# Who issues the shift copies of a convolution: SyncE in place of ScalarE in a Macaron state-space layer

## The chip, the cores and the metric

The kernel runs on one core of one Trainium2 chip. The metric is the device time of one execution in microseconds (us). A core has five engines that each work through an instruction list of their own, in order: TensorE (PE in the profile), VectorE (DVE), ScalarE (ACT), GpSimd (POOL) and SyncE (SP). They meet through semaphores. A DMA is issued by one of the engines; an engine's DMA issues stand in its own list, so a wait in front of a DMA holds up whatever is behind it on that engine.

## The reference

Input x has shape (2, 2048, 256), that is 4096 tokens of 256 channels. In short:

```
x = x + 0.5 * ffn(layernorm(x))      # 8 groups of 512 tokens, each with its own W1, b1, W2, b2; no nonlinearity
x = x + ssm(layernorm(x))
x = x + 0.5 * ffn(layernorm(x))

ssm(x): xz = x @ Wi.T + bi;  x_in, z = halves of xz (512 channels each)
        u  = silu(causal depthwise convolution of x_in with 4 taps + conv_b)
        dt = softplus(x_in[..., :32] @ Wdt.T + bdt)
        h  = h * exp(dt * A) + dt * Bm * u,  y = sum over 16 states of h * Cm     # along time
        out = (y * silu(z)) @ Wo.T + bo + x * Dv.mean()
```

## The kernel before

The tokens are cut into 4 iterations (`it`) of 1024 tokens, and the 512 channels into 4 tiles of 128 (`ct`). A block k = 4 * it + ct, from 0 to 15, is one tile of channels over one stretch of 1024 tokens. Block 0 is prepared in two halves of 512 tokens, and blocks 0 and 15 are scanned in two halves.

For each block the kernel makes these steps (stage names as in the code):

- `xim` on TensorE (x_in of the tile, two halves of 512 tokens in PSUM), `halo` and `xi` on ScalarE (three columns of the past, then bias and the copy into XI). XI has 128 partitions by two groups g of channels: group g fills the 64 partitions from 64 g on.
- `sh`: two DMAs that copy each group, shifted by one token, into the other 64 partitions of XI. So one matmul with a contraction over 128 partitions does two taps.
- `um` on TensorE (two taps at a time, DIAG as weights), `u` on ScalarE (silu). Likewise `zm` and `z`.
- `dm` on TensorE, `dtr`, `dte`, `dtl` on ScalarE and `dt` on VectorE make dt. `w` on VectorE makes dt * u. Both stand in DW.
- `repd` and `repw`: DMAs that spread a quarter q of the 128 channels over four times as many partitions, from DW to RD (dt) and to RV (dt * u). 512 KB each.
- 16 units per block, written (k, s), with the quarter q = s % 4: `exp` on ScalarE (G from RD), `scan` on VectorE (G from G and RV), and after each four scans `red` on TensorE (sum over states into Y). G has 8 buffers, so an exponential waits for the reduction of eight units earlier. `yz` on VectorE joins the block's Y with z.

Beside this run the norms (`sum`, `sq` and others), the FFN (the weights of each group are multiplied together first: `mm`, `ms`, `mv`, `mt`, `mtc`, with weights loaded by `wa`), the loads of X (`x`), the output projection (`opa`, `opm`, `op`) and the stores.

The order of all this is written by `schedule()`: a loop over the 288 units, with chains of steps that are let in at set points. It gives one list; each engine runs the stages of it that are its own, in that order. `proj(k)` puts `sh` in:

```
        do("xim", k, 1)
        yield 0
        do("xi", k, 1)
        do("sh", k)
        yield from rest_for(SHIFT)
```

Worked through, the list has these stages of SyncE on either side of `sh(k)` (w is repw, d is repd, numbers are block and quarter):

```
k    SyncE before            SyncE after
0    x(3)                    d(0), second half
1    w(0,3) second half      x(2), wa(20) to wa(27)
2    wa(27)                  d(1,0) to d(1,3), w(1,0) to w(1,3), wa(28) ...
3    w(2,1)                  w(2,2), w(2,3)
4    w(3,1), x(5)            w(3,2), w(3,3)
5    w(4,1)                  w(4,2), w(4,3)
6    w(5,1)                  w(5,2), w(5,3)
7    w(6,1), store(0)        w(6,2), w(6,3)
8    w(7,3)                  wa(52) to wa(59), w(8,0)
9    w(8,0)                  d(8,0) to d(8,3), w(8,1), wa(60) to wa(63), w(8,2)
10   w(9,1)                  w(9,2), w(9,3)
11   w(10,1), store(2)       w(10,2), w(10,3)
12   w(11,3)                 store(3), w(12,0)
13   w(12,1)                 w(12,2), w(12,3)
14   w(13,1)                 w(13,2), w(13,3)
15   w(14,1), store(4)       w(14,2), w(14,3)
```

On ScalarE `sh(k)` stands directly behind `xi(k,1)`. Behind `sh(1)` stands `sum(6)`, which reads x(2).

Of the kernel before, what the change touches and what calls it, by code (L numbers as in the profile page):

```python
# [12 lines left out]
TOK = 1024  # L13
# [39 lines left out]
HALVED, SPLIT = (0,), (0, 15)  # L53
# [37 lines left out]
def span(k, p):  # L91

    return (512 * p, 512 * p + 512) if k in HALVED else (0, TOK)
# [555 lines left out]
def build(nc, x, w, wit, wdt, wot, bo, cols, masks, out):  # L649
# [3 lines left out]
    with ctx:  # L653
        def sb(name, shape):
            return ctx.enter_context(nc.sbuf_tensor(name, shape, F32))
# [9 lines left out]
        XI = sb("XI", [P, 2, TOK + 3])  # L665
# [37 lines left out]
        sems = {name: ctx.enter_context(nc.semaphore("s_" + name)) for name in [*count.total, "skips", "mv1"]}  # L703
# [29 lines left out]
        def fourfold(v):  # L733

            return v.unsqueeze(1).broadcast_to([32, 4, v.shape[1]])

        def parts(i):

            k, p, s = UNITS[i]
            return k, p, s // 4, s % 4  # L740
# [19 lines left out]
        def scanned(k):  # L760

            return k, runs(k) - 1

        @block.sync
        def _(eng):
            e = Engine(eng, count, sems)

            def do(stage, *a):
                if stage == "x":
                    g, = a  # L770
                    if g >= NX:
                        e.wait_ge("store", g - NX)
                    eng.dma_start(X[:, g % NX, :, :], x[512 * g:512 * g + 512, :].rearrange("(i p) d -> p i d", p=P)
                                  ).then_inc(sems[DMA["x"](g)], 16)
                elif stage == "col":
                    eng.dma_start(COL[:, :], cols).then_inc(sems["col"], 16)
                elif stage == "mask":
                    eng.dma_start(MASKS, masks).then_inc(sems["mask"], 16)
                elif stage == "wdt":
                    eng.dma_start(WDT[:, :], wdt).then_inc(sems["wdt"], 16)  # L780
                elif stage == "bo":
                    eng.dma_start(BO[:, :], bo).then_inc(sems["bo"], 16)
                elif stage == "wi":
                    eng.dma_start(WI[:, :, :], wit.rearrange("(j p) n -> p j n", p=P)).then_inc(sems["wi"], 16)
                elif stage == "wo":
                    eng.dma_start(WO[:, :, :], wot.rearrange("(j p) n -> p j n", p=P)).then_inc(sems["wo"], 16)
                elif stage == "wh":
                    g, c = a
                    dst = heads[g][:, 513 * c:513 * (c + 2)].rearrange("p (k n) -> p k n", n=513)
                    eng.dma_start(dst, w[g].rearrange("(p k) n -> p k n", k=8)[:, c:c + 2, :]  # L790
                                  ).then_inc(sems[DMA["wh"](g, c)], 16)
                elif stage == "wa":
                    n, = a
                    if n - NW >= 16:
                        e.wait_ge("mm", n - NW)
                    eng.dma_start(W[:, n % NW, :], w[n // 8].rearrange("(p k) n -> p k n", k=8)[:, n % 8, :]
                                  ).then_inc(sems[DMA["wa"](n)], 16)
                elif stage == "store":
                    g, *part = a
                    pairs = part or (0, 1)  # L800
                    for pr in pairs:
                        e.wait_ge("ffn", g // 2, 1, g % 2, pr)
                    tiles = slice(2 * pairs[0], 2 * pairs[-1] + 2)
                    ov = out[512 * g:512 * g + 512, :].rearrange("(i p) d -> p i d", p=P)[:, tiles, :]
                    eng.dma_start(ov, X[:, g % NX, tiles, :]).then_inc(sems[DMA["store"](g)], 16)
                elif stage == "repd":
                    k, q, p = a
                    t0, t1 = span(k, p)
                    e.wait_ge("dt", k, p)
                    e.wait_ge("mm", 15)  # L810
                    if k:
                        e.wait_ge("exp", AT[(*scanned(k - 1), 12 + q)])
                    eng.dma_start(RD[:, q, t0:t1], fourfold(DW[q:P:4, 0, t0:t1])
                                  ).then_inc(sems[DMA["repd"](*a)], 16)
                elif stage == "repw":
                    k, q, p = a
                    t0, t1 = span(k, p)
                    e.wait_ge("w", k, p)
                    e.wait_ge("mm", 15)
                    n = 4 * k + q - NR  # L820
                    if n >= 0:
                        ko, qo = divmod(n, 4)
                        e.wait_ge("scan", AT[(*scanned(ko), 12 + qo)])
                    eng.dma_start(RV[:, (4 * k + q) % NR, t0:t1], fourfold(DW[q:P:4, 1, t0:t1])
                                  ).then_inc(sems[DMA["repw"](*a)], 16)
                elif stage == "end":
                    e.wait_ge("store", 6)
                    e.wait_ge("store", 7, 1)

            schedule(do)  # L830

        @block.gpsimd
# [68 lines left out]
        def _(eng):  # L901
            e = Engine(eng, count, sems)
            eng.preload_act_table_set("natural_log_exp_and_others")

            def do(stage, *a):
# [65 lines left out]
                elif stage == "ms":  # L971
                    g, = a
# [8 lines left out]
                elif stage == "mtc":  # L981
                    g, = a
# [44 lines left out]
                elif stage == "halo":  # L1027
                    k, = a
# [7 lines left out]
                elif stage == "xi":  # L1036
                    k, hf = a
# [6 lines left out]
                        ins = eng.activation(XI[ps, g, 3 + 512 * hf:515 + 512 * hf], bank("xim", k, hf)[ps, :],  # L1044
                                             ACT.Identity, bias=COL[ps, BI + k % 4:BI + k % 4 + 1])
                    ins.then_inc(sems["xi"])
                elif stage == "sh":
                    k, = a
                    e.wait_ge("halo", k)
                    e.wait_ge("xi", k, 1)  # L1050
                    c0 = 512 if k in HALVED else 0
                    for g in range(2):
                        eng.dma_start(XI[64 - 64 * g:128 - 64 * g, g, c0:TOK + 2],
                                      XI[64 * g:64 * g + 64, g, c0 + 1:TOK + 3]).then_inc(sems["sh"], 16)
                elif stage == "xd":
                    it, hf = a
                    ps = slice(32 * hf, 32 * hf + 32)
# [5 lines left out]
                elif stage == "u":  # L1063
                    k, hf = a
# [6 lines left out]
                elif stage == "z":  # L1071
                    k, hf = a
# [5 lines left out]
                elif stage == "dtr":  # L1078
                    k, hf = a
# [9 lines left out]
                elif stage == "dte":  # L1089
                    k, p = a  # L1090
# [6 lines left out]
                elif stage == "dtl":  # L1097
                    k, p = a
# [6 lines left out]
                elif stage == "save":  # L1105
                    i, = a
                    k, p, _ = UNITS[i]
# [3 lines left out]
                elif stage == "exp":  # L1111
                    i, = a
                    k, p, m, q = parts(i)
# [6 lines left out]
                    if o >= 0:  # L1120
                        e.wait_ge("red", o)
                        if kept(o):
                            e.wait_ge("save", o)
                    eng.activation(G[:, i % NG, t0:t1], RD[:, q, t0:t1], ACT.Exp,  # L1124
                                   scale=NAC[:, states(i):states(i) + 1]).then_inc(sems["exp"])

            schedule(do)

        @block.vector
# [376 lines left out]
```

## Time and profile before

| | |
|---|---|
| three timed runs, median | 760.28 us (758.97 to 765.12) |
| the profiled execution, its own time | 761.95 us |
| its span (first to last instruction) | 760.1 us |
| mean granted clock of TensorE | 0.926 of full |
| DMA issues of XI<-XI, all by ScalarE | 30 of 256.5 KB, 2 of 128.5 KB |
| DMA issues by SyncE | RD<-DW 68, RV<-DW 68, weights, X, stores |

All times of the trace are microseconds from the start of the span, from one execution. The line numbers are those of the kernel before.

### The profile page before, as it was taken

The page shows a single profiled execution, that of the slowest core. Times are in us where ns is not written, and L with a number is a line of the kernel's source. Part 1 is how long each engine was busy: PE and PEld are TensorE (multiplying, and loading weights), DVE is VectorE, ACT ScalarE, POOL GpSimd, SP SyncE. Part 2 cuts the span into 40 slices and gives each one's busy share as a digit, 9 for nine tenths or more (in the row PEclk, how much of TensorE's full clock was granted, in tenths as well). Part 3 has the DMA queues.
Part 4 walks back from the last instruction along what each step waited for, and adds up shares of the span by engine and source line. Part 5 has one row for each costly group of instructions (what it writes and reads, how often), then busy time and mean ns, then how long its engine had stood idle before and what let it go on. Part 6 is the DMA issues. An engine that isn't in the chain of part 4 may idle for free. (4 is left out here: it accounts for less than half of the span.)

```text
span 760.1 us, 8303 instructions
## 1 busy us (share of the span) xinstructions
PE 644.2 (85%) x2928; PEld 333.1 (44%) x2928; DVE 666.6 (88%) x450; ACT 607.4 (80%) x1074; POOL 293.8 (39%) x184
## 2 busy tenths in 40 slices
PE   7867786799896999979798999994977997798857
PEld 5632333364342466445144575531231553265435
DVE  2437947879999999999999999999999999999971
ACT  2488896879889989998788989898888787866663
POOL 0107020134344588479912565046970060600010
PEclk9997998989997899999899999997997999899879
DMA  8431465341838070431658070614234331605001
GB/s 294 148 138 43 164 225 164 133 172 32 320 104 315 7 245 5 160 117 49 227 150 301 34 236 0 231 47 166 84 146 132 139 111 71 206 28 221 1 1 55
DMA packets 40026, 103.08 MB, mean 136 GB/s; under 512 B 4080, under 2 KB 13040, under 8 KB 39984
## 3 DMA queue, kind: packets, MB, share of 16 engines
q1 hardware_dynamic: 37424, 94.40, 34.2%
q10 hardware_dynamic: 2560, 8.14, 4.6%
q8 instruction: 23, 0.38, 0.2%
q14 instruction: 19, 0.16, 0.1%
HBM read 23.08 MB, written 4.19 MB: 36 GB/s over the span
## 5 line engine op out<-in xcount | busy, mean ns | idle before, releaser
L1124 ACT ACTIVATE G<-RD,COL 128x1024 f32<-128x1024 f32 (+1 forms) x288 | 280.0, 1042 | 56.2 <-PE Y L1424 50.8
L1246 DVE TENSOR_TENSOR_SCAN G<-G,STT,RV 128x1024 f32<-128x1024 f32 (+1 forms) x160 | 312.5, 2016 | 1.5 <-ACT G L1124 1.5
L1246 DVE TENSOR_TENSOR_SCAN G<-G,RV 128x1024 f32<-128x1024 f32 (+1 forms) x128 | 268.7, 2155 | 13.9 <-ACT G L1124 13.8
L1424 PE MATMUL Y<-G,RW 128*32 128x512 f32 x1024 | 144.6, 682 | 49.4 <-DVE G L1246 46.1
L849 POOL TENSOR_SCALAR LV<-LV 128x4 f32<-128x4 f32 x18 | 17.3, 962 | 226.4 <-ACT XN L944 226.1
L858 POOL TENSOR_TENSOR LV<-LV,HALF 128x4 f32<-128x4 f32 (+1 forms) x25 | 47.8, 1913 | 135.8 <-DVE LV L1201 134.3
L1424 PEld LDWEIGHTS Y<-G,RW 128*32 128x32 f32 x1024 | 28.0, 117 | 127.6 <-DVE G L1246 64.6
L875 POOL TENSOR_SCALAR XN<-X,LV 128x256 f32<-128x256 f32 x36 | 75.9, 2113 | 1.9
L1391 PE MATMUL MB<-XI,DIAG 128*64 128x512 f32 x248 | 64.3, 656 | 12.7 <-DMA XI<-XI 10.8
L1350 PE MATMUL MB<-MT,XF 128*128 128x256 f32 x240 | 59.6, 393 | 9.9 <-ACT MT L986 7.6
L1369 PE MATMUL MB<-XT,WI 128*128 128x512 f32 x128 | 63.4, 624 | 3.7 <-ACT XT L970 3.7
L889 POOL TENSOR_SCALAR X<-X,LV 128x256 f32<-128x256 f32 x32 | 65.2, 2047 | 0.8
L1448 PE MATMUL MB<-WO,ZS 128*128 128x256 f32 x256 | 64.0, 383 | 0.0
L1402 PE MATMUL MB<-XT,WI 128*128 128x512 f32 x128 | 59.7, 615 | 4.0 <-ACT XF L970 2.6
L895 POOL TENSOR_SCALAR MS<-MS,MV 128x256 f32<-128x256 f32 x12 | 27.4, 2290 | 88.3 <-DVE MV L1178 88.3
L1350 PEld LDWEIGHTS MB<-MT,XF 128*128 128x128 f32 x240 | 46.9, 198 | 18.8 <-ACT MT L986 6.0
L1448 PEld LDWEIGHTS MB<-WO,ZS 128*128 128x128 f32 x256 | 49.3, 192 | 6.8
L1287 PE MATMUL MB<-W 128*128 128x257 f32 x192 | 47.8, 396 | 1.4 <-DMA W<-in_w 1.4
L944 ACT ACTIVATE XN<-X,LV 128x256 f32<-128x256 f32 x96 | 47.5, 498 | 1.6 <-DVE LV L1206 1.1
L1044 ACT ACTIVATE XI<-MB,COL 64x512 f32<-64x512 f32 x64 | 43.3, 676 | 3.5 <-PE MB L1369 3.1
L1287 PEld LDWEIGHTS MB<-W 128*128 128x128 f32 x192 | 35.5, 194 | 20.1 <-issue 10.5
L1194 DVE SCALAR_TENSOR_TENSOR DW<-MB,COL,DW 128x1024 f32<-128x1024 f32 (+1 forms) x18 | 20.5, 1143 | 25.1 <-ACT DW L1102 25.1
(96 smaller groups left out, 779.7 us busy)
## 6 DMA issues: line engine op xcount, KB each, us to landing
RD<-DW SPq DMA_DIRECT2D x60, 512.0 KB, 3.7
RV<-DW SPq DMA_DIRECT2D x60, 512.0 KB, 4.9
W<-in_w SPq DMA_DIRECT2D x48, 256.5 KB, 3.6
XI<-XI ACTq DMA_DIRECT2D x30, 256.5 KB, 5.6
X<-in_x SPq DMA_DIRECT2D x8, 512.0 KB, 6.3
out<-X SPq DMA_DIRECT2D x7, 512.0 KB, 3.3
G<-in_w SPq DMA_DIRECT2D x4, 513.0 KB, 8.4
RV<-in_w SPq DMA_DIRECT2D x4, 513.0 KB, 12.3
```

The source lines that it names most:

```text
L858: eng.tensor_tensor(lv[:, 3, ts], lv[:, 1, ts], HALF[:, ts], ALU.pow).then_inc(sems["rstd"])
L875: ins = eng.tensor_scalar(xn[:, i, :], v[:, i, :], lv[:, 3, i:i + 1], lv[:, 4, i:i + 1], ALU.mult, ALU.add)
L889: eng.tensor_scalar(v[:, i, :], v[:, i, :], lv[:, 5, i:i + 1], lv[:, 6, i:i + 1], ALU.mult, ALU.add).then_inc(sems["skip"])
L1124: eng.activation(G[:, i % NG, t0:t1], RD[:, q, t0:t1], ACT.Exp, scale=NAC[:, states(i):states(i) + 1]).then_inc(sems["exp"])
L1246: eng.tensor_tensor_scan(g, g, RV[:, (4 * k + q) % NR, t0:t1], STT[:, idx:idx + 1] if goes_on else 0.0, ALU.mult, ALU.add).then_inc(sems[" ...
L1287: ins = eng.matmul(bank("merge", g, i)[:, 0:257], v[:, 257 + 128 * i:385 + 128 * i], v[:, 0:257], start=(c == 0), stop=(c == 7))
L1350: ins = eng.matmul(o, xf[:, j, 128 * t:128 * t + 128], MT[:, g % NX, j, :], start=False, stop=(i == 1 and j == 1))
L1369: ins = eng.matmul(bank("xim", k, hf), WI[:, j, 128 * ct:128 * ct + 128], XT[:, j, 512 * hf:512 * hf + 512], start=(j == 0), stop=(j == 1))
L1391: ins = eng.matmul(bank("um", k, hf)[64 * g:64 * g + 64, :], DIAG[:, 4 * ct + 2 * g + t, :], XI[:, g, 512 * hf + 2 * t:512 * hf + 2 * t + ...
L1402: ins = eng.matmul(bank("zm", k, hf), WI[:, j, 512 + 128 * ct:640 + 128 * ct], XT[:, j, 512 * hf:512 * hf + 512], start=(j == 0), stop=(j ...
L1424: ins = eng.matmul(Y[32 * q:32 * q + 32, 512 * h:512 * h + 512], RW[:, states(i + o), :], G[:, (i + o) % NG, 512 * h:512 * h + 512], start ...
L1448: ins = eng.matmul(o, ZS[:, (4 * it + ct) % NZ, 128 * (2 * pr + i):128 * (2 * pr + i) + 128], WO[:, ct, :], start=False, stop=(i == 1 and ...
```

## The change

The stage `sh` moves from ScalarE's list to SyncE's, at the same place in the order. Its waits (`halo`, `xi`), its two DMAs, their sizes and their semaphore stay; no other stage changes.

```diff
         @block.sync  (do)
+                elif stage == "sh":
+                    k, = a
+                    e.wait_ge("halo", k)
+                    e.wait_ge("xi", k, 1)
+                    c0 = 512 if k in HALVED else 0
+                    for g in range(2):
+                        eng.dma_start(XI[64 - 64 * g:128 - 64 * g, g, c0:TOK + 2],
+                                      XI[64 * g:64 * g + 64, g, c0 + 1:TOK + 3]).then_inc(sems["sh"], 16)
         @block.scalar  (do)
-                elif stage == "sh":
-                    k, = a
-                    e.wait_ge("halo", k)
-                    e.wait_ge("xi", k, 1)
-                    c0 = 512 if k in HALVED else 0
-                    for g in range(2):
-                        eng.dma_start(XI[64 - 64 * g:128 - 64 * g, g, c0:TOK + 2],
-                                      XI[64 * g:64 * g + 64, g, c0 + 1:TOK + 3]).then_inc(sems["sh"], 16)
```

## Rows read from the trace of the kernel before

**Rows 1.** The page's first part: busy us (share of the span) xinstructions.

```profile
PE 644.2 (85%) x2928; PEld 333.1 (44%) x2928; DVE 666.6 (88%) x450; ACT 607.4 (80%) x1074; POOL 293.8 (39%) x184
```

**Rows 2.** Windows, 600 to 690 us: stretch, length, busy us of each engine, clock, DMA.

```profile
600.00:690.00 90.00, 80.76 (x380) 44.04 (x377) 90.00 (x47) 71.53 (x105) 25.62 (x12) 0.94 0.35 125
```

**Rows 3.** Timeline of VectorE: start, us, line, what, [idle before <-releaser].

```profile
104.15 1.28 DVE L1194 SCALAR_TENSOR_TENSOR DW<-MB,COL,DW 128x1024 f32<-128x1024 f32 x1 [10.19 <-ACT DW L1102]
...
118.45 8.84 DVE L1246 TENSOR_TENSOR_SCAN G<-G,RV 128x1024 f32<-128x1024 f32 x4 [4.78 <-ACT G L1124]
...
144.53 1.23 DVE L1233 TENSOR_TENSOR DW<-DW 128x1024 f32<-128x1024 f32 x1 [3.46 <-ACT DW L1069]
...
166.56 4.53 DVE L1246 TENSOR_TENSOR_SCAN G<-G,RV 128x1024 f32<-128x1024 f32 x2 [5.51 <-ACT G L1124]
...
352.80 4.59 DVE L1246 TENSOR_TENSOR_SCAN G<-G,STT,RV 128x1024 f32<-128x1024 f32 x2 [1.49 <-ACT G L1124]
```

**Rows 4.** The line that issues sh: ns min/median/max, first and last start.

```profile
L1053 ACTq DMA_DIRECT2D XI<-XI x32: 468/564/2587, 67.4 to 653.2; - x32
```

**Rows 5.** Timeline of SyncE's and ScalarE's issues and one sum, 80 to 114 us.

```profile
80.68 0.60 SPq L773 DMA_DIRECT2D X<-in_x  x1
...
92.78 1.12 ACTq L1053 DMA_DIRECT2D XI<-XI  x2
93.94 0.42 ACT L919 ACTIVATE XN<-X 128x256 f32<-128x256 f32 x1 [1.25 <-issue]
...
105.46 3.39 SPq L813 DMA_DIRECT2D RD<-DW  x4
...
113.75 3.08 ACTq L1053 DMA_DIRECT2D XI<-XI  x2
```

**Rows 6.** Issue to landing: X at 80.7, XI at 210.3, RD burst, XI at 113.7.

```profile
DMA to landing us min/median/max: 3.6/3.6/3.6
...
DMA to landing us min/median/max: 3.1/3.4/3.8
...
L813 SPq DMA_DIRECT2D RD<-DW x4: 530/706/1318, 105.5 to 107.5; - x4
DMA to landing us min/median/max: 3.0/4.2/4.8
...
DMA to landing us min/median/max: 6.5/7.9/9.4
```

**Rows 7.** Timeline of block 1: TensorE's um(2,0), ScalarE's exponentials of units 8 on.

```profile
123.73 3.68 PE L1391 MATMUL MB<-XI,DIAG 128*64 128x512 f32 x8 [6.13 <-DMA XI<-XI]
...
137.60 3.23 ACT L1124 ACTIVATE G<-RD,COL 128x1024 f32<-128x1024 f32 x3 [0.95 <-PE Y L1424]
```

**Rows 8.** Timeline around block 3: VectorE's scans, SyncE's RV, ScalarE's XI.

```profile
202.69 13.63 DVE L1246 TENSOR_TENSOR_SCAN G<-G,RV 128x1024 f32<-128x1024 f32 x6
...
202.95 1.82 SPq L824 DMA_DIRECT2D RV<-DW  x2
...
210.25 1.12 ACTq L1053 DMA_DIRECT2D XI<-XI  x2
```

**Rows 9.** Timeline around block 8: RD, XI, exponentials of units 0 to 3, dt.

```profile
399.45 3.59 SPq L813 DMA_DIRECT2D RD<-DW  x4
...
405.49 1.26 ACTq L1053 DMA_DIRECT2D XI<-XI  x2
...
408.55 4.27 ACT L1124 ACTIVATE G<-RD,COL 128x1024 f32<-128x1024 f32 x4 [1.15 <-PE Y L1424]
...
418.31 1.25 DVE L1194 SCALAR_TENSOR_TENSOR DW<-MB,COL,DW 128x1024 f32<-128x1024 f32 x1
```

**Rows 10.** Timeline around block 6: RV(6,2) and (6,3), XI, scan (6,2).

```profile
321.62 2.65 SPq L824 DMA_DIRECT2D RV<-DW  x2
...
325.52 1.41 ACTq L1053 DMA_DIRECT2D XI<-XI  x2
...
334.32 2.34 DVE L1246 TENSOR_TENSOR_SCAN G<-G,STT,RV 128x1024 f32<-128x1024 f32 x1
```

## The prediction

> **What bounds the kernel now.** The page's first part gives the busy shares: VectorE 88%, TensorE 85%, ScalarE 80% [rows 1]. The windows by stage say more than the average: from 600 to 690 us VectorE is busy for 90.00 of 90.00 us [rows 2]. It runs the 288 scans one behind the other, and a microsecond in which a scan is late there is a microsecond of the span. So I listed VectorE in order of time and looked for its gaps [rows 3]. Before the first full-width scan (block 1, at 118.45) there are large ones, 10.19 and 4.78 us. Inside block 1 there are 3.46 and 5.51 us. From 166.56 until after 690 us few are left, the largest 1.49 us at 352.80. That gives two rules for costing a delay. Up to 166 us it counts where it lies on the chain that ends a gap. After that it counts almost whole as soon as it reaches a scan.
>
> **What is moved.** 32 DMA issues of ScalarE, 0.468 to 2.587 us each, median 0.564 [rows 4]: 32 x 0.564 = 18 us of ScalarE's time at the least. The bytes, the two waits and the place in the order stay. What changes is the engine that stands still until `xi(k,1)` is done. ScalarE never stood still for it, for it makes XI itself. SyncE does, and everything queued behind `sh(k)` on SyncE stands with it: input tiles, weights, and the replications RD and RV from which ScalarE and VectorE live. So for each of the 16 pairs I took the time of the issue on ScalarE (XI is ready just before it) and laid it beside the time at which SyncE issued the next item of its own order. Where SyncE's item came earlier, it is now late by the difference plus the two issues. On ScalarE an undisturbed pair takes 1.12 us [rows 5]; I use 1.15.
>
> **Step 1, sh(1), in front of x(2).** SyncE issued x(2) at 80.68; XI is ready at 92.7, where ScalarE issues the pair (92.78), and the next thing ScalarE does is the sum over x(2), at 93.94 [rows 5]. Now x(2) is issued at 92.75 + 1.15 = 93.9. Alone it took 3.6 us to land, the XI pair 3.1 to 3.8 us from issue, and four 512 KB replications of one burst 3.0 to 4.8 us [rows 6]. The last of that burst landed at 107.5 + 4.8 = 112.3 and the first at 105.5 + 3.0 = 108.5, so each further 512 KB costs (112.3 - 108.5)/3 = 1.28 us. The second of the XI pair lands at 93.3 + 3.8 = 97.0, x(2) 1.28 us later at 98.3; with no such queueing at 93.9 + 3.6 = 97.5. ScalarE's sum starts at 98.3 instead of 93.94: 4.4 us late (3.6 to 6). All that follows on ScalarE up to the dt step of block 1 is without a gap, and VectorE stands in its 10.19 us gap waiting for just that [rows 3]. So +4.4 goes to everything behind. The weights wa(20) to wa(27) also move behind x(2), but TensorE needs them some 2 us before ScalarE's late chain needs their product: nothing, and 1 to 2 us if that cover is thin.
>
> **Step 2, sh(2), in front of the replications of block 1.** In the frame of the old times (all 4.4 us later): SyncE issued repd(1) at 105.46 and XI is ready at 113.66, the pair being issued at 113.75 [rows 5]. Now the pair goes at 113.7, repd(1,0) at 114.9. The second XI lands at 114.2 + 3.8 = 118.0, and repd(1,0) to (1,3) and repw(1,0) follow in the same queue: 118.0 + 5 x 1.28 = 124.4, and 126.5 if the queue is a third slower under such a load (1.7 us each). The first scan of block 1 needs repw(1,0), so it starts at 124.4 and not at 118.45. Most of this has cover. Block 1 has gaps of 3.46 and 5.51 us, 9 us together, and they hang on another chain: TensorE waited 6.13 us for the late landing of sh(2), and ScalarE's exponentials of units 8 to 11 began at 137.60 [rows 7]. The pair meets no other traffic now and lands 5 us earlier, so TensorE and its weight products are early. What releases those exponentials then is the scans: four (8.84 us), the yz product (1.17), the reduction on TensorE (2.0) behind the first scan's start, so 124.4 + 12.1 = 136.5, or 138.6 at the upper bound, against 137.60. The next group, eight scans in, gives 146.6 to 148.8 against 147.2. So block 2 starts 0.6 us earlier to 1.6 us later: I take +0.5. ScalarE's long issue there (3.08 us for the pair) is gone too, but it lay under this wait.
>
> **Step 3, sh(4), in front of repw(3,2).** SyncE issued repw(3,2) at 202.95; the pair was issued at 210.25 [rows 8]. Now repw(3,2) goes at 211.4. VectorE's run of six scans from 202.69 holds the last two of block 2 and the first four of block 3, at 2.27 us each [rows 8], so scan (3,2) starts at 202.69 + 4 x 2.27 = 211.8. Its operand lands 1.28 us after the second XI (214.5 + 1.3 = 215.8), at the least 211.4 + 3.0 = 214.4 (the quickest of the burst [rows 6]). VectorE stands for 2.6 to 4.0 us: +3.5, nearer to the upper end, since the pair is always just ahead in the queue. There is no gap near it to take this up.
>
> **Step 4, sh(9), in front of repd(8).** repd(8) was issued from 399.45 on and the pair at 405.49 [rows 9]. Now repd(8,0) goes at 406.65, and the four land at about 411.0 to 414.9. ScalarE's exponentials of units 0 to 3, begun at 408.55, end one exponential (1.07 us) behind the last landing, at 416.0 instead of 412.8. The dt chain of block 9 behind them takes 3.5 us and ends at 419.5, where VectorE took it up at 418.31 [rows 9]: 1.2 us, or nothing if the four land 1.2 us sooner. +1.0.
>
> **The other twelve.** In seven of them (k = 0, 6, 8, 10, 12, 13, 14) SyncE has nothing due before XI is ready. For k = 3, 5, 7, 11 and 15 a repw (.,2) is late by 0.2 to 5 us. The tightest is k = 7: repw(6,2) at 321.62 becomes 326.65, for the pair went at 325.52. It lands at 331.4, and scan (6,2) starts at 334.32 [rows 10]: 2.9 us of cover, and 3 to 10 us in the other four. Nothing; if ScalarE were 3 us later against the scans, each microsecond beyond would count.
>
> **What ScalarE gets back.** Its 18 us lie mostly in front of waits for TensorE's reduction, which come from the scans. They count where ScalarE itself ends a gap of VectorE: 1.49 us at 352.80 [rows 3], on a stretch without waits behind the pair of 325.52 (1.41 us [rows 10]), and smaller gaps at 502 and 507, 1.2 us together. At most 2.7 us; I take half: -1.4.
>
> The Trainium skill, "DMA: Bandwidth & Descriptors", section "Issuing engines are not separate DMA queues", says that DMAs of scalar, sync and gpsimd all run on the same 16 engines and interleave, and that another issuer only saves issue time on a sequencer. The landing of 9.4 us for sh(2) beside a SyncE burst, against 3.8 for sh(4) [rows 6], agrees with the sharing. By that rule alone only the term of ScalarE's issue time would stand and the sum would be slightly negative, which is the second rival below; the rule is silent on the items behind a blocked sequencer.
>
> **The sum.** 4.4 + 0.5 + 3.5 + 1.0 - 1.4 = 8.0 us. Span 760.1 + 8.0 = 768.1 us. The profiled execution took 761.95 us, 1.85 more than its span, and lies 1.7 us above the median of the three timed runs (760.28); added to the median the change gives 768.3 us, +1.05%. About 1% is what a measurement of this kernel can tell from no change, so the forecast lies on that bound.
>
> **Rivals.**
> Absorbed: the first delay hides. ScalarE, TensorE and VectorE are all idle for parts of the stretch up to 166 us, and if x(2) lands sooner or block 1's gaps (9 us) take up step 1 as well, steps 1 and 2 come to 0 to 2 us. With step 3: +2 to +4, 762 to 764 us. For: the gaps are large. Against: ScalarE's chain from 93.94 is closed.
> Relief, the other side: SyncE's blocking costs nothing and ScalarE's 18 us come back. This decides if the operands on which steps 1 and 3 rest are not waited for, that is if XI is ready before about 89 us for x(2) and 207 us for repw(3,2). Then -1.4 to -2.7 us from the gaps that ScalarE ends, 757.6 to 759 us; up to -8 if the exponentials run ahead everywhere. Against: in this trace XI is ready at 92.7 and 210.2.
> Cascade: each stall leaves TensorE idle too, the granted clock falls, and blocks behind it run late, so that repw(6,2) and its like lose their 3 us. Block 1 at the upper bounds (+1.6), step 1 at 6, another 3 us at one more block: +13 to +18, 773 to 778 us.
>
> **Chances.** As worked out (764 to 773 us) 0.63; absorbed 0.17; cascade 0.13; relief 0.07. The range to hold 8 in 10 reaches from the absorbed case to the lower half of the cascade, 762.5 to 775. Slower by over 1% (above 767.9) is half of the main case and a bit, and the cascade: 0.50. Faster by over 1% is a small part of the relief: 0.04. The rest, 0.46, is within 1%.
>
> **What would show it.** Right: x(2) issued near 93.9 and a wait of ScalarE for the DMA of X in front of the sum; the first scan of block 1 at about 129 with block 2 starting near 171; a gap of VectorE of 3 to 4 us in front of scan (3,2), which ends with a DMA of RV; near 352.8 a smaller gap. Wrong: if XI is ready sooner on SyncE's side than on ScalarE's old place, if a single queue drains faster or slower than 1.28 us for 512 KB, or if a later block loses its cover.

## The result and the profile after

The changed kernel takes 781.15 us (median of 4 runs) against 761.19 us before: ratio 1.0254, 95% interval 1.0207 to 1.0301. It is 2.5% slower. The forecast was 768.3 us, in a range of 762.5 to 775. Medians, here and below, are of all executions; ratios leave out those more than 1.5% above the fastest of their kernel (two of these ran at a granted clock of 0.81 and 0.82 instead of about 0.93). The profiled execution has a span of 778.9 us, 18.8 more than before.

The first part of the page of the kernel after, and its DMA queue of SyncE, beside [rows 1]:

```profile
PE 650.3 (83%) x2928; PEld 337.1 (43%) x2928; DVE 667.3 (86%) x450; ACT 609.0 (78%) x1074; POOL 295.5 (38%) x184
...
q1 hardware_dynamic: 39984, 102.54, 37.3%
```

VectorE's work is the same (667.3 us for 666.6). What grew is its idle time. SyncE's queue now carries the pairs too: 102.54 MB and 37.3% of the engines' span, where it was 94.40 MB and 34.2%. The waits of SyncE's own queue say where to look (what waited, for what, us in total, times, longest):

```profile
SPq L181 <- ACT XI L1052: 94.4, 13, 19.8
```

Line 181 is the wait of the stages, so SyncE stood for 94.4 us in front of `sh`, in 13 waits. The question is which of it anybody else felt. VectorE in order of time, kernel after, beside [rows 3]:

```profile
113.78 1.28 DVE L1194 SCALAR_TENSOR_TENSOR DW<-MB,COL,DW 128x1024 f32<-128x1024 f32 x1 [18.96 <-ACT DW L1102]
134.75 8.84 DVE L1246 TENSOR_TENSOR_SCAN G<-G,RV 128x1024 f32<-128x1024 f32 x4 [11.45 <-DMA RV<-DW]
...
224.70 4.47 DVE L1246 TENSOR_TENSOR_SCAN G<-G,RV 128x1024 f32<-128x1024 f32 x2 [4.40 <-DMA RV<-DW]
...
433.78 4.48 DVE L1246 TENSOR_TENSOR_SCAN G<-G,RV 128x1024 f32<-128x1024 f32 x2 [0.70 <-DMA RV<-DW]
451.17 4.71 DVE L1246 TENSOR_TENSOR_SCAN G<-G,RV 128x1024 f32<-128x1024 f32 x2 [1.64 <-ACT G L1124]
...
478.42 1.41 DVE L1194 SCALAR_TENSOR_TENSOR DW<-MB,COL,DW 128x512 f32<-128x512 f32 x2 [1.43 <-ACT DW L1102]
485.10 1.22 DVE L1255 TENSOR_TENSOR ZS<-ZS,Y 128x1024 f32<-128x1024 f32 x1 [2.42 <-PE Y L1424]
```

The four places of the prediction are there. The gap in front of dt(1) grew from 10.19 to 18.96 us. The first scan of block 1 waits for RV (11.45 us), and the two gaps inside block 1, 3.46 and 5.51 us before, have shrunk to nothing and 0.75. The gap in front of scan (3,2) is 4.40 us. The surprise is the third stretch: from block 8 into block 9 there are six gaps, 7.5 us together, where the kernel before has one of 1.16.

To cost them I numbered the 288 scans in both profiles (a merged row of n scans divided evenly) and took, for each, how much later it starts than in the kernel before. The differences of this column between two places are what the stretch costs. All runs stand here, in us against the first profile of the kernel before:

| start of scan, later than before by | block 0, 2nd half | its unit 11 | block 1 | block 2 | block 4 | block 8 | block 10 | block 15, 2nd half |
|---|---|---|---|---|---|---|---|---|
| after (all by SyncE) | 0.8 | 9.6 | 16.3 | 8.2 | 12.9 | 12.8 | 19.2 | 17.4 |
| the kernel before again | 2.3 | 2.9 | 2.9 | 2.8 | 2.9 | 3.8 | 3.5 | 3.6 |
| only sh(1) | 2.3 | 10.7 | 8.9 | 7.8 | 7.9 | 10.6 | 10.4 | 10.5 |
| only sh(2) | -0.1 | 0.4 | 6.7 | -2.2 | -1.9 | -2.2 | -2.2 | -2.3 |
| only sh(4) | 0.2 | 0.7 | -1.1 | -1.3 | 5.2 | 5.0 | 4.8 | 4.8 |
| only sh(9) | -2.0 | -2.0 | -2.5 | -2.2 | -2.2 | -1.1 | 5.3 | 5.6 |
| the other twelve | -1.0 | -0.1 | -1.8 | -2.7 | -2.7 | -2.8 | -3.0 | -4.8 |
| SyncE waits only | -0.4 | 7.1 | 13.7 | 5.6 | 9.9 | 8.0 | 16.6 | 16.0 |
| x(2) first | -2.6 | 3.3 | 10.0 | 1.9 | 8.5 | 6.4 | 12.5 | 10.6 |
| x(2), wa(20) to wa(23) first | 1.5 | 1.4 | 7.7 | -0.8 | 4.1 | 3.8 | 10.2 | 8.2 |
| sh(9) behind RD | 2.1 | 2.7 | 0.9 | 0.8 | 0.9 | -1.9 | -2.1 | -2.2 |
| by SyncE, in the order of readiness | 0.2 | -0.3 | -3.2 | -2.3 | -2.3 | -4.3 | -3.2 | -4.9 |

Read along a row, not down a column: the first column is what the start-up happened to take in that execution (-2.6 to +2.3 us), before anything changed has an effect. In the kernel after the start-up took 0.8 us more, the stretches cost 8.8 us (sh(1)), -1.4 (sh(2)), +4.7 (sh(4)), 0, +6.4 (sh(9)) and -1.8, and the last blocks add 1.4 to the span's 18.8.

### The profile page after: what moved, and what is told of

Read it like the earlier page. It is cut to its first block and busy times, and to the rows that moved or that the text cites. A ratio compares the mean times of both kernels' runs of the same rounds, so it can differ in the third digit from the quotient of the medians.

```text
span 778.9 us, 8303 instructions
## 1 busy us (share of the span) xinstructions
PE 650.3 (83%) x2928; PEld 337.1 (43%) x2928; DVE 667.3 (86%) x450; ACT 609.0 (78%) x1074; POOL 295.5 (38%) x184
## 3 DMA queue, kind: packets, MB, share of 16 engines
q1 hardware_dynamic: 39984, 102.54, 37.3%
## 5 line engine op out<-in xcount | busy, mean ns | idle before, releaser
L1424 PE MATMUL Y<-G,RW 128*32 128x512 f32 x1024 | 146.7, 691 | 57.8 <-DVE G L1246 53.1
L866 POOL TENSOR_TENSOR LV<-LV,HALF 128x4 f32<-128x4 f32 (+1 forms) x25 | 45.7, 1830 | 138.6 <-DVE LV L1201 137.1
L897 POOL TENSOR_SCALAR X<-X,LV 128x256 f32<-128x256 f32 x32 | 70.6, 2217 | 0.8
L1391 PE MATMUL MB<-XI,DIAG 128*64 128x512 f32 x248 | 61.1, 628 | 8.1 <-DMA XI<-XI 4.6
L903 POOL TENSOR_SCALAR MS<-MS,MV 128x256 f32<-128x256 f32 x12 | 30.2, 2526 | 98.2 <-DVE MV L1178 98.2
L1287 PE MATMUL MB<-W 128*128 128x257 f32 x192 | 54.4, 436 | 12.9 <-DMA W<-in_w 12.9
L883 POOL TENSOR_SCALAR XN<-X,LV 128x256 f32<-128x256 f32 x36 | 64.0, 1783 | 1.9
L1287 PEld LDWEIGHTS MB<-W 128*128 128x128 f32 x192 | 39.7, 216 | 33.6 <-DMA W<-in_w 17.4
```

The lines of the kernel that those rows point to most:

```text
L883: ins = eng.tensor_scalar(xn[:, i, :], v[:, i, :], lv[:, 3, i:i + 1], lv[:, 4, i:i + 1], ALU.mult, ALU.add)
L897: eng.tensor_scalar(v[:, i, :], v[:, i, :], lv[:, 5, i:i + 1], lv[:, 6, i:i + 1], ALU.mult, ALU.add).then_inc(sems["skip"])
L1287: ins = eng.matmul(bank("merge", g, i)[:, 0:257], v[:, 257 + 128 * i:385 + 128 * i], v[:, 0:257], start=(c == 0), stop=(c == 7))
L1391: ins = eng.matmul(bank("um", k, hf)[64 * g:64 * g + 64, :], DIAG[:, 4 * ct + 2 * g + t, :], XI[:, g, 512 * hf + 2 * t:512 * hf + 2 * t + ...
L1424: ins = eng.matmul(Y[32 * q:32 * q + 32, 512 * h:512 * h + 512], RW[:, states(i + o), :], G[:, (i + o) % NG, 512 * h:512 * h + 512], start ...
```

## The experiments

**One place at a time.** A constant says which pairs SyncE issues; the rest stay with ScalarE.

```diff
+BY_SYNC = (1,)          # and (2,), (4,), (9,), or the twelve others
 @block.sync
+                elif stage == "sh" and a[0] in BY_SYNC:
 @block.scalar
-                elif stage == "sh":
+                elif stage == "sh" and a[0] not in BY_SYNC:
```

> Only sh(1) by SyncE, the other fifteen by ScalarE as before. Theory A (the items queued behind the blocked SyncE cost the time, x(2) and the weights wa(20) on): x(2) is issued near 94 to 96 us, ScalarE waits about 5 to 6 us for it in front of the sum and about 3 us for the reduction behind late weights, and the scan of unit 11 of block 0's second half starts about 9 us later than before; of that some 4 to 8 us reach the end of the span. Rival B (it is the traffic of all sixteen pairs in SyncE's one DMA queue that slows every landing): one pair alone does next to nothing, under 2 us. Rival C (the gaps of block 1 take the delay up): 9 us at unit 11, but 0 to 2 us at the start of block 2 and at the end.

> Only sh(2) by SyncE. Theory A: the first scan of block 1 starts 6 to 7 us later than before, and the start of block 2 lies within -1.5 to +1.5 us of before, because the gaps of 3.5 and 5.5 us in block 1 hang on the landing of sh(2), which comes 5 us sooner. Total -1.5 to +1.5 us. Rival C (a late first scan of block 1 goes to the end whole): +6 to +7 us. Rival B: under 1 us anywhere.

> Only sh(9) by SyncE. Theory A: RD of block 8 is issued 6 to 7 us late, the weight loads wa(60) to wa(63) reach the queue 1 to 2 us late and TensorE waits about 4 to 5 us for them in front of a reduction; VectorE loses 4 to 6.5 us between the start of block 8 and unit 4 of block 9. Rival (as predicted blind: only the dt step of block 9 is late): +1 us. Rival B: under 1 us.

> All pairs but 1, 2, 4 and 9 by SyncE. Theory A: no operand of a scan is late, and the relief of ScalarE shows where ScalarE ended a gap of VectorE (1.5 us at 352.8, 1.2 us near 502 to 507): -3 to 0 us against before. Rival B (traffic in one queue): several us slower, in proportion to the twelve pairs, 5 to 9 us. Rival (a later block loses its cover, such as repw(6,2) with 2.9 us): +1 to +3 us in that block.

> Only sh(4) by SyncE. Theory A: repw(3,2) is issued 8 to 9 us later, VectorE waits 3.5 to 4.5 us for it in front of unit 2 of block 3, and all of it reaches the end, since no gap lies near: +3.5 to +4.5 us against the same place of the kernel before. Rival C (taken up by later gaps): under 1.5 us at the end.

| by SyncE | this, us | before, us | ratio (95%) |
|---|---|---|---|
| only sh(1) | 771.58 | 760.70 | 1.0140 (1.0069 to 1.0211) |
| only sh(2) | 759.68 | 760.70 | 0.9998 (0.9962 to 1.0033) |
| only sh(4) | 767.66 | 762.47 | 1.0076 (1.0036 to 1.0116) |
| only sh(9) | 773.49 | 760.70 | 1.0175 (1.0088 to 1.0261) |
| the other twelve | 759.23 | 760.70 | 0.9974 (0.9942 to 1.0006) |

Three of sixteen pairs make the whole loss. sh(1) costs 8.4 us at unit 11 in the table and 8.2 at the end, sh(9) 6.4 and sh(4) 6.5 where they lie. The twelve, with three quarters of the traffic, are no slower: against the theory that one queue for everything is what costs.

sh(2) delays the first scan of block 1 by 6.4 us and still leaves block 2 2.6 us earlier than it would have been. That it gains anything is not shown, though. From the same unit 11 to block 2 kernels that leave sh(2) with ScalarE are ahead too, by 2.9 us (only sh(1)), 2.6 (the other twelve), 2.0 (only sh(4)) and 1.9 (sh(9) behind RD), and only sh(9) and the second profile of the kernel before are not (0.2 and 0.1). What goes with it is the length of ScalarE's second issue of that pair: 2.59 and 2.56 us in the two profiles of the kernel before, 2.02 with only sh(9), 0.72 to 0.79 in the other four. What makes it long is not shown. sh(2) on SyncE costs nothing; that much stands.

Three expectations missed. sh(1) came to 10.9 us in the timed runs, where 4 to 8 were expected. sh(9) came to 12.8, where 4 to 6.5 were expected; its profile, with 5.1 us more span than the first of the kernel before, is of the fastest of its four executions (766.99 us, the others 771.90 to 775.37), so 5 to 8 us of the others' time are in no trace. And sh(4) costs 6.5 where it lies; I expected 3.5 to 4.5, the size in the kernel after. The profile of only sh(4) shows what the size hangs on:

```profile
203.55 4.27 ACT L1133 ACTIVATE G<-RD,COL 128x1024 f32<-128x1024 f32 x4 [4.63 <-PE Y L1433]
...
211.13 1.15 SPq L813 DMA_DIRECT2D XI<-XI  x2
...
212.33 1.95 SPq L833 DMA_DIRECT2D RV<-DW  x2
...
217.05 4.47 DVE L1255 TENSOR_TENSOR_SCAN G<-G,RV 128x1024 f32<-128x1024 f32 x2 [6.42 <-DMA RV<-DW]
```

ScalarE's exponentials waited 4.63 us for the reduction, where they waited 3.15 in the kernel before and after. XI of block 4 stands behind them, so the pair went 2.0 us later against the scans (0.5 us behind the end of the last one, in the kernel after 1.5 us ahead of it), and the gap was 6.42 us instead of 4.40. The 1.5 us of the wait are TensorE's clock. In all three kernels it stands idle for 2.68 us in front of the four matmuls ahead of that reduction; they take 1.95 and 1.96 us in the kernel before and after, at a granted clock of 1.00 (2.4 GHz), and 3.44 us with only sh(4), at 0.55 (most of it at the lower level, 1.2 GHz). With x(2) first (below) it is the same: 2.87 us for the four and 2.65 for the reduction (1.92 otherwise), a wait of 4.79 and a gap of 6.30. What decides the level there is open. The price of a blocked queue moves one for one with the engine that releases it.

**The wait alone.** SyncE waits at the sixteen places, and ScalarE issues the pairs as before.

```diff
 @block.sync
+                elif stage == "sh":
+                    e.wait_ge("halo", *a)
+                    e.wait_ge("xi", *a, 1)
```

> SyncE only waits for halo and xi at the sixteen places, the pairs are issued by ScalarE as before. Theory A (it is the wait on SyncE, not where the DMA is issued): most of the loss of the full change returns, +12 to +20 us (no relief of ScalarE; the items behind are free one pair of issues earlier, 1.15 us, but sh and they then share the engines). Rival B (the transfers in SyncE's queue): within 2 us of before.

780.87 against 762.47 us, ratio 1.0245 (1.0200 to 1.0290), beside 1.0254 for the full change. The pairs still move, but in ScalarE's queue; no byte of XI is in SyncE's, and the loss is all there. So it is not the pairs' place in SyncE's queue that costs; the position of the wait is.

**What is in step 1.** All by SyncE, but sh(1) behind x(2), and behind x(2) and wa(20) to wa(23).

```diff
 @block.sync
             def do(stage, *a):
+                if stage == "sh" and a[0] in BEHIND:
+                    return
+                act(stage, *a)                      # what do() was
+                for k, item in BEHIND.items():      # BEHIND = {1: ("x", 2)} or {1: ("wa", 23)}
+                    if item == (stage, *a):
+                        act("sh", k)
```

> All by SyncE as in the full change, but x(2) goes ahead of sh(1). Theory A with two parts of the first step, x(2) for ScalarE's sum (5 to 6 us) and the weights wa(20) on for the reduction (3 us, and more if the sum no longer covers them): the sum starts without a wait, TensorE still waits about 5 to 6 us for the weights in front of the reduction, and of the 9 us of the first step about 2 to 4 us go: total +14 to +17 us. Rival (x(2) is all of the first step): total +9 to +11 us.

> All by SyncE as in the full change, but sh(1) goes behind x(2) and wa(20) to wa(23). Theory A (the first step is x(2) plus the weights): TensorE's wait for W in front of the reduction goes too, unit 11 of block 0's second half starts 0 to 1.5 us later than before instead of 9, and the total is 8 to 10 us below that of the full change: +9 to +11 us. Rival (the rest of the first step is something else than the weights): no better than x(2) first alone, +13 to +15 us.

776.98 us against 762.47, ratio 1.0190 (1.0145 to 1.0234), and 770.94 against 759.25, ratio 1.0137 (1.0091 to 1.0184). The totals are +14.5 us (forecast 14 to 17) and +11.7 (forecast 9 to 11, a little short). With x(2) first, 5.9 of the 8.8 us of the first step stay. The trace of that kernel names their cause: the weights.

```profile
96.72 3.43 PE L1305 MATMUL MB<-W 128*128 128x257 f32 x8 [4.97 <-DMA W<-in_w]
...
101.21 2.56 ACT L1142 ACTIVATE G<-RD,COL 128x512 f32<-128x512 f32 x4 [6.71 <-PE Y L1442]
```

TensorE waits 4.97 us for a weight tile, and the eight matmuls behind the wait take 3.43 us, at a granted clock of 0.58. Behind them stands the reduction that frees G, and ScalarE waits 6.71 us for it. With four weight loads in front as well, TensorE does not wait, the same eight take 2.00 us, and the step is gone (1.5 to 1.4 in the table).

**What is in step 4.** Only sh(9) by SyncE, behind the four RD of block 8.

> Only sh(9) by SyncE, behind the four RD of block 8 instead of in front of them. Theory A (the loss in block 8 comes through RD being late and, behind RD, the weights wa(60) to wa(63)): both are on time or 1 us late, and of the 6.5 us lost with sh(9) in front 0 to 1.5 us are left. Rival (the pair's own landing by SyncE is what TensorE waits for): 4 us or more are left.

761.61 against 759.25 us, ratio 1.0022 (0.9982 to 1.0062), and from block 8 to 10 the table shows -1.9 and -2.1: nothing is lost. In the kernel with sh(9) in front (first three rows) the late RD is only the first link; the second is again a weight tile and the reduction behind it. With RD first (last row) TensorE's wait is 1.77 us, and its eight matmuls take 2.00 us instead of 3.80:

```profile
409.68 1.15 ACT L1133 ACTIVATE G<-RD,COL 128x1024 f32<-128x1024 f32 x1 [5.51 <-DMA RD<-DW]
...
416.38 3.80 PE L1296 MATMUL MB<-W 128*128 128x257 f32 x8 [5.49 <-DMA W<-in_w]
...
422.18 3.23 ACT L1133 ACTIVATE G<-RD,COL 128x1024 f32<-128x1024 f32 x3 [3.80 <-PE Y L1433]
```

```profile
410.60 2.00 PE L1305 MATMUL MB<-W 128*128 128x257 f32 x8 [1.77 <-DMA W<-in_w]
```

**The kernel before once more.**

> The kernel before once more, for what two profiles of the same kernel differ by. Both theories: the scans start within 2 us of the first profile. The gap of 1.49 us at 352.80 decides a side question: if it is ScalarE's issue of sh(7) that makes it, it is there again; if it comes and goes by itself, it may be gone, with about 1.3 us more at unit 9 of block 7.

One execution, 765.11 us, span 763.3. The gap of 1.49 us at 352.80 is not in this profile of the same kernel; instead block 7 has two that the first profile has smaller or not at all:

```profile
396.71 1.28 DVE L1194 SCALAR_TENSOR_TENSOR DW<-MB,COL,DW 128x1024 f32<-128x1024 f32 x1 [0.34 <-ACT DW L1102]
399.35 1.22 DVE L1233 TENSOR_TENSOR DW<-DW 128x1024 f32<-128x1024 f32 x1 [1.35 <-ACT DW L1069]
...
511.08 6.92 DVE L1246 TENSOR_TENSOR_SCAN G<-G,RV 128x1024 f32<-128x1024 f32 x3 [0.67 <-ACT G L1124]
```

So that gap comes and goes by itself and says nothing of ScalarE's issues. The last row is another matter. This gap and its two neighbours (0.52 and 0.39 us, at 505.82 and 522.37) are in both profiles of the kernel before and in those of only sh(1), sh(2), sh(4), sh(9) and sh(9) behind RD, and in none of the kernels in which SyncE issues sh(11): after, the other twelve, the first-step kernels and the next one. That is the relief: 1.6 us of gaps, and 1.7 to 2.0 us in the table between block 10 and block 15. Some of it goes again behind the table's last column: one gap in block 15 is 0.72 us in the kernel before and 1.92 in the kernel after. It is as long with sh(9) behind RD, where ScalarE issues fifteen of the pairs, so what makes it is open.

**Every pair where SyncE is free.** All sixteen by SyncE, eight of them moved behind the stages that were due earlier.

```diff
+BEHIND = {1: ("wa", 23), 2: ("repw", 1, 3, 0), 3: ("repw", 2, 2, 0), 4: ("repw", 3, 3, 0), 7: ("repw", 6, 3, 0),
+          9: ("repw", 8, 1, 0), 11: ("repw", 10, 3, 0), 15: ("repw", 14, 3, 0)}
```

> All by SyncE, but eight pairs moved behind those SyncE stages that were due before XI was ready: sh(1) behind wa(23), sh(2) behind repw(1,3), sh(3) behind repw(2,2), sh(4), sh(7), sh(11), sh(15) behind the repw of quarter 3, sh(9) behind repw(8,1). Theory A: nothing is late any more and ScalarE keeps its relief: -4 to 0 us against before. Rival B (one queue for all traffic is slower as such): +3 us or more. Rival (sh(2) behind eight replications lands as late as before or later, near 9 to 11 us, and holds TensorE in block 1): +1 to +3 us at the start of block 2.

757.45 against 762.47 us, ratio 0.9937 (0.9912 to 0.9962): faster than the kernel before by 0.6%, with the whole interval below 1, but by less than the 1% that the prediction took for what can be told, and the lowest ratio here (its interval overlaps that of the other twelve). SyncE issues the same 32 DMAs as in the kernel that is 2.5% slower. In block 1 ScalarE no longer stands in a 3.08 us issue, so the first scan waits 1.84 us for RV where it waited 4.78 for ScalarE, though sh(2) lands hardly sooner and TensorE still waits 5.20 us for it. Of these 2.9 us only some 1.1 can be put down to the move: where ScalarE's issue of the pair takes 1.3 us, as with the other twelve, the wait is 2.99 already.

```profile
115.22 8.84 DVE L1264 TENSOR_TENSOR_SCAN G<-G,RV 128x1024 f32<-128x1024 f32 x4 [1.84 <-DMA RV<-DW]
```

```profile
122.51 3.68 PE L1409 MATMUL MB<-XI,DIAG 128*64 128x512 f32 x8 [5.20 <-DMA XI<-XI]
```

## Why the prediction was wrong

The sign was right, and so was the first link of the mechanism: the items behind the blocked SyncE, at the four places named. The sum was 8.0 us; 18.8 came. Two terms were far too small, steps 1 and 4, and for the same reason: weight loads behind the pair, put at nothing in one and not listed in the other, stopped TensorE, which then also ran at half its clock. The terms:

**Step 1: 4.4 forecast, 8.8 measured. This step failed on its last sentence**, "the weights ... nothing, and 1 to 2 us if that cover is thin". The kernel after:

```profile
94.48 1.14 SPq L812 DMA_DIRECT2D XI<-XI  x2
95.66 0.61 SPq L773 DMA_DIRECT2D X<-in_x  x1
96.31 13.47 SPq L796 DMA_DIRECT2D W<-in_w  x8
100.72 0.42 ACT L927 ACTIVATE XN<-X 128x256 f32<-128x256 f32 x1 [6.32 <-DMA X<-in_x]
...
102.18 3.80 PE L1287 MATMUL MB<-W 128*128 128x257 f32 x8 [6.59 <-DMA W<-in_w]
...
107.57 2.56 ACT L1124 ACTIVATE G<-RD,COL 128x512 f32<-128x512 f32 x4 [2.93 <-PE Y L1424]
```

The sum's wait was forecast as 98.3 - 92.7 = 5.6 us and is 6.32 (x(2) took 5.0 us to land, not 4.4). Then ScalarE meets a second wait, 2.93 us, for a reduction that stands on TensorE behind matmuls that wait 6.59 us for weights. I had compared the weights with the step that reads their product, and not with what else is queued behind those matmuls. x(2) first leaves 5.9 us of the step, x(2) and the weights first none.

Most of the second wait is TensorE's clock. After 6.59 us of waiting the eight matmuls take 3.80 us, at a granted clock of 0.50 from 102.2 to 106.0 (the lower level, 1.2 GHz), and the reduction behind them takes 1.59, at 0.75 from 106 to 108. In the kernel before TensorE works on without a wait there, at 1.00 (2.4 GHz):

```profile
93.80 2.00 PE L1287 MATMUL MB<-W 128*128 128x257 f32 x8
95.73 1.06 PE L1424 MATMUL Y<-G,RW 128*32 128x512 f32 x8
```

That is 2.3 us of the 2.93; the late weights alone would have left 0.6 (an estimate from these rows).

**Step 2: +0.5 forecast, -1.4 measured** in the full change, -2.6 alone. The bounds were -0.6 to +1.6 (its 8.84, 1.17 and 2.0 make 12.0, not 12.1). Against the kernels in which ScalarE's issue of sh(2) is short the step is near nothing, as shown above. In the kernel with sh(2) alone the first scan stands behind a gap of 11.13 us, 6.4 us later than before and about as worked out (5.9), and TensorE's wait for sh(2) fell from 6.13 to 0.97 us. That TensorE then also keeps its pace was not counted: the eight matmuls behind that wait take 1.94 us there and 3.68 us before [rows 7], in the same shape. Before, the granted clock from 124 to 128 us was 0.50, the lower of its two levels (1.2 GHz), after 6.13 us of waiting; here it was 1.00 from 118.9 to 121 us, the upper one (2.4 GHz).

```profile
118.93 1.94 PE L1400 MATMUL MB<-XI,DIAG 128*64 128x512 f32 x8 [0.97 <-DMA XI<-XI]
```

**Step 3: 3.5 forecast, 4.4 to 4.7 measured**, the gap itself 4.40 us. The range 2.6 to 4.0 was short because RV landed 4.7 to 5.2 us from its issue behind the pair. Alone it was 6.5 us, with TensorE at the lower clock ahead of it, as shown above.

**Step 4: +1.0 forecast, +6.4 measured. The second failure, of the same kind.** The forecast of the first link held: RD to ScalarE at 411.0 in the old frame, 423.8 with the 12.8 us of shift, measured 423.39. The weight loads in SyncE's order behind repw(8,1) were not in the step at all. The kernel after:

```profile
417.52 1.11 SPq L812 DMA_DIRECT2D XI<-XI  x2
418.72 4.27 SPq L821 DMA_DIRECT2D RD<-DW  x4
423.04 1.34 SPq L832 DMA_DIRECT2D RV<-DW  x1
423.39 4.89 ACT L1124 ACTIVATE G<-RD,COL 128x1024 f32<-128x1024 f32 x4 [5.32 <-DMA RD<-DW]
424.43 3.32 SPq L796 DMA_DIRECT2D W<-in_w  x4
429.84 3.79 PE L1287 MATMUL MB<-W 128*128 128x257 f32 x8 [4.81 <-DMA W<-in_w]
...
436.10 4.27 ACT L1124 ACTIVATE G<-RD,COL 128x1024 f32<-128x1024 f32 x4 [4.33 <-PE Y L1424]
```

They were issued 1.8 us late (424.43, against 409.78 + 12.8) and into a queue still full, so they landed in 4.8 to 5.4 us where it was 2.8 to 4.0. TensorE waited 4.81 us and then ran at a granted clock of 0.50 from 429.8 to 433.6: 3.79 us for eight matmuls that take 2.00 in the kernel before, and 2.45 us for the reduction instead of 1.92. So the reduction came late, by 2.3 us more than the wait, then the exponentials, and VectorE paid in six small gaps up to unit 4 of block 9. Nowhere is one gap larger than 2.42 us. The kernel before at that place:

```profile
412.83 2.00 PE L1287 MATMUL MB<-W 128*128 128x257 f32 x8 [0.48 <-DMA W<-in_w]
414.76 1.92 PE L1424 MATMUL Y<-G,RW 128*32 128x512 f32 x16
```

**The other twelve: 0 forecast**, and shown: no scan of theirs is late.

**The relief: -1.4 forecast, -1.8 measured, but partly by luck.** It comes from the gaps near 502 to 519 alone, and block 15 gives 1.2 us of it back. The 1.49 us at 352.80, on which the forecast leaned, vanish in a second profile of the unchanged kernel too.

**The rivals.** Relief fell (it decides if XI is ready early, and it was not). Absorbed held for step 2 only. Cascade came nearest in size. Its first half was right: a stall left TensorE idle, and the granted clock fell, which cost 2.3 us of ScalarE's wait in step 1 and as much of TensorE's time in step 4. Its second half was not: repw(6,2) kept its cover. And what stopped TensorE, weight loads in the same queue, it did not name. The Trainium skill, "DMA: Bandwidth & Descriptors", section "Issuing engines are not separate DMA queues", has a second issuer save only a sequencer's time. The runs agree on the transfers (SyncE's waits with the pairs left in ScalarE's queue cost 1.0245, the full change 1.0254) and add what the sentence leaves out: where the issuer waits decides 3% between two kernels with the same DMAs on the same queue, 1.0254 and 0.9937.

What stays open: singly the three bad places cost 8.2, 4.6 and 7.6 us at the last column, with sh(2) and the twelve taking 2.2 and 3.8 back: 14.4 us, and together 16.6. The rest of 2.2 us is of the size by which two profiles of one kernel differ. The timed medians do not add up so well: 10.9, 5.2 and 12.8 us less 1.0 and 1.5 make 26.4, against 20.0 for the full change, and most of that excess is the part of only sh(9) that no trace shows. Nor did any run hold TensorE's clock up while the weights were late, so the clock's share is read from rows, not from an experiment.

## What to carry to other kernels

A DMA issue that waits for an engine belongs on a queue where nothing behind it is due before that engine is done; list, for the queue it moves to, every item behind it with its due time, small weight loads too. Then follow each late operand to the instruction that waits for it, and go on to what stands behind that instruction on its engine: the prices here, waits of 2.9 and 4.3 us on ScalarE, came by a reduction that had nothing to do with the late tile. If that engine is TensorE, look at its granted clock behind the wait: here eight matmuls took 3.8 us instead of 2.0 after 6.6 and 4.8 us of standing idle. If the order can be chosen, put the waiting issue behind the items already due; that turned a ratio of 1.0254 into 0.9937.

## What the runs showed that I had not expected

Two profiles of the same kernel differ by 3.2 us in span (760.1 and 763.3), 2.3 us of it before 83 us, and by single gaps of 1 to 1.5 us (at 352.80) that come and go. A term of that size worked out from one gap of one profile is not yet a term. And the four RD replications behind a pair in one queue reached ScalarE 1.36 us apart (129.33 to 133.40 in block 1 of the kernel after), close to the 1.28 us worked out from a burst before: that figure carried over well, and what failed was the list of who was in the queue.
